# Moving the running counts of a second expert router from VectorE to GpSimd

## What is computed

```python
x = x + _L1_xattn_ref(_layernorm(x, axis=-1), ctx_768, ...)
x = x + _L1_ffn_ref(_layernorm(x, axis=-1), L1_ffn_Wg, ...)

scores = jax.nn.softmax(xf @ Wg.T, axis=-1)
expert_weights, expert_indices = jax.lax.top_k(scores, K)
expert_weights = expert_weights / expert_weights.sum(-1, keepdims=True)
gates = (jax.nn.one_hot(expert_indices, E, dtype=xf.dtype) * expert_weights[..., None]).sum(axis=1)
```

## Time and profile before

| | |
|---|---|
| time, median of 3 runs | 917.48 us (917.41 to 917.69) |
| time of the profiled execution | 909.81 us |
| its span, first to last instruction | 908.6 us |
| mean granted TensorE clock | 0.868 |
| TensorE busy | 707.4 us (78% of the span) |
| VectorE busy | 677.9 us (75%) |
| GpSimd busy | 565.0 us (62%) |
| ScalarE busy | 472.4 us (52%) |

### The profile page before, as it was taken

How to read it: one execution, slowest core, us unless ns; L and a number is a source line. 1 busy time by engine, 2 the same in 40 slices (tenths; PEclk the granted TensorE clock), 3 DMA queues, 4 the chain that set the end, 5 groups by cost and what they waited for, 6 DMA issues and landing times. The chain is left out here.

```text
span 908.6 us, 21071 instructions
## 1 busy us (share of the span) xinstructions
PE 707.4 (78%) x6384; PEld 522.0 (57%) x6384; DVE 677.9 (75%) x3212; ACT 472.4 (52%) x1318; POOL 565.0 (62%) x932
## 2 busy tenths in 40 slices
PE   0697898899888899943798269988888865899960
PEld 0364565566686566422575256666666642799960
DVE  6798999999447887686111294798998886699964
ACT  3466666765303554520233464777777741677740
POOL 7688977786647443201777684347777767377770
PEclk9879999998999999976899655998988876899985
DMA  6300123777227877500564500000000013799918
GB/s 147 59 25 9 41 49 63 90 93 100 41 47 282 268 253 253 180 1 7 76 122 114 181 28 1 3 2 23 23 26 25 23 34 118 212 274 266 266 53 277
DMA packets 98830, 94.43 MB, mean 104 GB/s; under 512 B 37511, under 2 KB 82302, under 8 KB 98142
## 3 DMA queue, kind: packets, MB, share of 16 engines
q1 hardware_dynamic: 91268, 79.34, 33.1%
q0 software_dynamic: 6592, 13.58, 6.0%
q10 hardware_dynamic: 858, 0.17, 0.1%
HBM read 47.76 MB, written 43.19 MB: 100 GB/s over the span
## 5 line engine op out<-in xcount | busy, mean ns | idle before, releaser
L2455 POOL DMA_INDIRECT expert_pairs<-e_ys,e_home x78 | 75.4, 967 | 38.4 <-issue 23.5
L1791 POOL TENSOR_SCALAR a_kb<-a_kr,a_m,a_bk 128x128 f32<-128x128 f32 x128 | 57.8, 452 | 44.4 <-ACT a_kr L2032 32.3
L1809 POOL DMA_INDIRECT expert_slots<-r_rows,r_slotu x64 | 63.3, 990 | 30.2 <-DVE r_rows L2189 15.1
L961 DVE MATCH_REPLACE8 work<-m,work 128x64 f32<-128x64 f32 x384 | 75.6, 206 | 0.0
L1533 POOL DMA_INDIRECT ex_rows<-rows,slot_source x32 | 30.7, 961 | 53.3 <-POOLq L1176 43.9
L948 DVE MAX8 m<-work 128x8 f32<-128x64 f32 x384 | 57.0, 208 | 0.0
L1864 PE MATMUL a_pss<-a_kb,a_qt 32*64 32x256 f32 x512 | 41.5, 463 | 13.8 <-ACT a_pp L2017 11.7
L2221 DVE TENSOR_REDUCE a_mx<-a_pss 128x8 f32<-128x512 f32 x64 | 43.8, 685 | 8.1 <-PE a_pss L1864 7.8
L2422 PE MATMUL e_ps<-e_XH,e_wh 128*128 128x256 f32 x156 | 48.1, 308 | 1.5 <-DVE e_XL L2467 1.5
L1585 ACT ACTIVATE ex_hs<-ex_psh,vec 128x512 f32<-128x512 f32 x32 | 22.0, 687 | 49.8 <-PE ex_psh L1566 49.1
L2424 PE MATMUL e_ps<-e_XH,e_wl 128*128 128x256 f32 x156 | 44.6, 286 | 0.0
(11 more groups left out here) (477 smaller groups left out, 2469.5 us busy)
## 6 DMA issues: line engine op xcount, KB each, us to landing
expert_slots<-rt_unfilled SPq DMA_DIRECT2D x151, 130.0 KB, 2.6
ahead<-folded_weights SPq DMA_DIRECT2D x20, 386.0 KB
e_wf<-folded_weights SPq DMA_DIRECT2D x19, 386.0 KB, 4.1
planes<-rt_zeros SPq DMA_DIRECT2D x4, 1024.0 KB
ew<-in_L_ffn_ew SPq DMA_DIRECT2D x16, 256.0 KB, 3.8
pair_y<-expert_pairs SPq DMA_DIRECT2D x16, 256.0 KB, 5.2
e_xr<-expert_slots SPq DMA_DIRECT2D x27, 130.0 KB, 3.2
folded_weights<-fold_done SPq DMA_DIRECT2D x8, 384.0 KB, 4.3
```

Of the source, the lines that this page charges most:

```text
L961: return own.did(dve.match_replace(wk_[x.j][:, h, :], m8[x.j][:, h, r, :], src[:, h, :], TAKEN))
L1791: m = pool.tensor_scalar(kb[a.j][:, :, h, :], k, m4[:, h:h + 1], bk4[:, h:h + 1], ALU.mult, ALU.add)
L1809: pool.indirect_dma_start(G.slots, bass.IndirectOffsetOnAxis(ap=slot[:, b, k, t:t + 1], axis=0), rb[b % NB][:, k, t, :], None).then_inc(se ...
L2455: pool.indirect_dma_start(G.pair, bass.IndirectOffsetOnAxis(ap=home[i % NY][:, k:k + 1], axis=0), ys[i % NY][:, k, :], None).then_inc(kept ...
```

## The change

The four adds become a function `running_counts`. For blocks 0 to 5 GpSimd calls it, at the head of its slot `PLACE`, before the scaled keys, after a wait for the new semaphore `r_chosen`, which VectorE's last instruction on `sel` raises. For blocks 6 and 7 VectorE still makes the adds. The memset of the first count goes to GpSimd too.

```diff
+        def running_counts(eng, step, b):
+
+            for t in range(b * TB, (b + 1) * TB):
+                m = eng.tensor_tensor(run[:, t + 1, :], run[:, t, :], full["sel"][:, t, :], ALU.add)
+                if t + 1 < (b + 1) * TB:
+                    step.then(m)
+            m.then_inc(r["sel"], 1)
...
                 pool.sem_inc(s["zero"], 1)
+                step.did(pool.memset(run[:, 0, :], 0.0))
...
                 def slot_of(x):
                     a = x.by(3)
+                    counted = due(x, PLACE)
+                    if counted is not None:
+                        pool.wait_ge(r["chosen"], counted + 1)
+                        after(pool, r["sel"], counted)
+                        running_counts(pool, step, counted)
                     if a.real():
                         pool.wait_ge(s["k_sb"], a.t + 1)
...
-                dve.memset(run[:, 0, :], 0.0)
...
                 def choose_second(b):
                     w = part(b)
                     largest(b, 1)
-                    step.then(TT(w["sel"], oh[:, b, 0, :, :], oh[:, b, 1, :, :], ALU.add))
-                    for t in range(b * TB, (b + 1) * TB):
-                        m = TT(run[:, t + 1, :], run[:, t, :], full["sel"][:, t, :], ALU.add)
-                        if t + 1 < (b + 1) * TB:
-                            step.then(m)
-                    m.then_inc(r["sel"], 1)
+                    TT(w["sel"], oh[:, b, 0, :, :], oh[:, b, 1, :, :], ALU.add).then_inc(r["chosen"], 1)
+                    if b >= LAST - 1:
+                        dve.wait_ge(r["chosen"], b + 1)
+                        after(dve, r["sel"], b)
+                        running_counts(dve, step, b)
                     step.then(TT(w["d"], w["m1"], w["m0"], ALU.subtract))
```

More of the change, by code:

```diff
@@ L1673, in combination_and_second_attention @@
         r = {n: C.sem("r2_" + n) for n in (
-            "iota", "lg", "var", "root", "rows", "d", "exp", "sel", "ranks", "pos", "counted",
+            "iota", "lg", "var", "root", "rows", "d", "exp", "chosen", "sel", "ranks", "pos", "counted",
             "slot", "gs", "gturned", "gt", "bias", "bias_sum", "dve", "table")}
```

## The result

The changed kernel takes 935.45 us, the median of 4 runs (929.21 to 938.2), against 917.59 for the kernel before (917.41 to 922.72). The ratio is 1.0171 with a 95% interval of 1.0107 to 1.0236: slower by 15.7 us, between 9.8 and 21.7. The forecast was 930.9, +13.4.

What follows compares the result with a forecast made beforehand. Four engines share the stage, VectorE busiest, but GpSimd reaches the adds after TensorE's ranks want them. Block 1's 2.17 plus 11.2 us over four later periods gave 13.4 on 917.48: 930.9 us, range 926.0 to 937.0.

Steps and rivals of the forecast that it cites:

- the head: Point where GpSimd ends a block's last send; 0.89 to 1.49 us after TensorE's ranks in blocks 1 to 5.
- The ring: Loop from GpSimd's first send through its work, adds, ranks and next send: 26.64 us against 23.85; chance 0.84.
- GpSimd's wait of 2.03 us: GpSimd's wait for VectorE's rows before block 2's first send; claimed not to pay for the adds.
- The term of block 1: Block 1's ranks move from 634.93 to 637.10, waiting for GpSimd's adds: +2.17 us.
- Adds and release: GpSimd's four adds, 1.13 us, plus 0.15 until TensorE's ranks start: 1.28 us.
- Ranks to send: From TensorE's ranks to GpSimd's next first send: 5.63 us at the slow clock, 4.86 for block 1.
- Send to next head: GpSimd's work from a block's first send to the end of its last: 19.73 us without a wait.
- the TensorE rival: TensorE's clock stays low for whole blocks, four slots making 29.8 us: 27 us in all, 944 us; chance 0.06.
- The gain costed at nothing: VectorE's adds removed in blocks 0 to 5, 5.6 us, gain nothing; in blocks 1 to 5 its reciprocal awaits the projection.
- Faster: Adds leave the busiest engine and GpSimd is ready in time: gain up to 5.6 us, 912 us; chance 0.05.
- Absorbed: Adds of 1.13 us fit in GpSimd's 2.03 us wait, nothing moves: 917.5 us within 1.8; chance 0.05.
- Dear adds: GpSimd's adds take 1.0 us more in each of five blocks: +5.0, 935.9 us; within range, no separate chance.

Runs made afterwards that it cites:

- e5: Kernel before, VectorE keeping its adds; a GpSimd memset at its slot PLACE raises a semaphore that the ranks of blocks 0 to 5 also await; ratio 1.0111.
- e3: Kernel before, VectorE keeping its adds; GpSimd also makes the same four adds in slot PLACE, into a tile nothing reads; ratio 0.9949.
- e4: Changed kernel with GpSimd's adds one slot earlier, behind the keys and ahead of the previous block's last sends; ratio 0.9997.
- e1: Changed kernel run once more, unaltered; ratio to the kernel before 1.0162.
- e8: Kernel before, with VectorE's four adds of blocks 0 to 5 done twice, the extra ones into a tile nothing reads; ratio 0.9996.
- e12: Second run of e8's kernel, VectorE's adds of blocks 0 to 5 done twice against the kernel before; ratio 1.0020.
- e7: The change for block 3 alone, VectorE adding in all other blocks; 927.86 us against 919.82 for the kernel before.
- e9: Kernel before, with TensorE's input projections moved between the two halves of the scores; ratio 1.0018 from four of twelve runs, median of all twelve 935.05 us.
- e2: Kernel before, with a bare semaphore increment on GpSimd's queue in slot PLACE that the ranks also wait for; ratio 1.0006.
- e11: Kernel before, unaltered, for a second profile; first sends of blocks 0 to 5 lie 118.48 us apart, one run.

## Why the prediction was right

**The place of the loss: right, and shown.** Ranks behind the head in blocks 1 to 5, none in block 0; e5 has most of the loss (8.55 us) without the adds on GpSimd, e3 the adds there without the loss, and e4 has them there in time, without the loss. The ring was part of the prediction; that GpSimd's wait of 2.03 us does not pay for the adds is borne out too, since that wait grew to 3.49.

**The term of block 1 (+2.17).** +2.00 in after's profile, +2.63 in e1's.

**The ring (+2.79, four times: 11.2).** +11.95 in after and +9.93 in e1. The three parts of 26.64 were each nearly right, with errors that cancel in part:

- Adds and release, 1.28 taken: 1.13 in every block. The adds took 1.05 for 1.08, and TensorE followed 0.06 us behind GpSimd's last add; I had taken 0.15 from a wait of TensorE for VectorE. The Trainium skill (GPSIMD Engine Reference, section 3.1) measures a GpSimd add at 1.96 times VectorE's duration for 2048 columns. That ratio does not hold at 8 columns here: an add took 0.204 us on GpSimd, and on VectorE, before, 0.166 as the median and 0.202 as the mean of 24, so the ratio is 1.2 by the median and 1.0 by the mean.
- Ranks to send, 5.63 taken: 5.50 to 5.53, and 4.79 in the block of each profile where the clock was up for part of it (4.86 had been taken for block 1).
- Send to next head, 19.73 taken as unbroken work: 19.79 in block 1, but 20.31, 20.27 and 20.40 after that. Here is the part of the TensorE rival that I had left inside the range. In the slot behind the ranks TensorE is still at its lower clock (granted 0.50 from 676.46 to 679.90), VectorE's next reciprocal comes late, and GpSimd waits for the statistics that VectorE writes after it. In e1 this is seen in one period only (20.24; the others are 19.7 to 19.8). VectorE's and GpSimd's timelines, after:

```profile
679.90 0.96 DVE L2284 RECIPROCAL a_rt<-a_pso 128x128 f32<-128x128 f32 x1 [1.68 <-PE a_pso L1945]
```

```profile
681.43 0.25 POOL L1783 TENSOR_SCALAR r_v<-r_mv 128x4 f32<-128x4 f32 x1 [0.54 <-DVE r_mv L2255]
```

The clock over the whole distance is 0.79, for 0.86 before.

**The gain costed at nothing: right for this change.** In the profile after, VectorE waits 3.2 to 4.5 us for TensorE before the reciprocal of blocks 1 to 5, so its freed 0.93 us could only lengthen that wait. Beyond this change it is open what VectorE's time is worth: e4 cannot show it, since its own ring holds the period at 23.97, and e8 and e12 disagree. Nor is 23.85 us what the other engines need per block. e7 shows 22.6 to 22.8 with VectorE's adds in place, so the period of before is not a floor; it contains a slow slot of TensorE around each block's ranks. The windows (columns of the earlier trace rows) of that slot in before, and of the ranks to send of block 2 in e7:

```profile
655.60:662.40 6.80, 6.25 (x80) 4.83 (x78) 5.92 (x20) 4.29 (x14) 4.90 (x9) 0.50 0.07 22
```

```profile
668.90:674.40 5.50, 4.47 (x57) 3.16 (x54) 5.23 (x18) 3.98 (x13) 3.90 (x7) 0.93 0.08 27
```

That the slow slot sets the 23.9 fits these two, but e9, meant to show it, changed more than the clock, and e3 speaks against its simplest form: its clock is 0.93 in every one of the five periods, and they are 23.7 to 23.9 all the same. What sets the period of the kernel before stays open.

**The rivals.** Faster fell: no profile shows it. Absorbed fell as the way the change behaves, though e3 shows that its arithmetic (1.1 us fit in 2.03) was true; what it missed is who waits. TensorE as the bound came in part, as above, not as 29.8 us per block (four slots of 7.4 are 29.6, a slip that changes no chance). Dear adds fell: an add took 0.204 us for the 0.21 taken.

**The size.** 13.4 predicted; 13.95 and 12.56 in the two profiled distances; 15.7 (9.8 to 21.7) and 14.9 (9.3 to 20.4) in time. The agreement within 1 us owes something to errors of opposite sign, in the ring and, in e1, between block 1 and the ring. The statement that a measurement can tell 0.2% from no change was wrong: the three runs then known lay 0.3 us apart, but the interval came out at 0.6% to either side. The median of 935.45 lies inside 926 to 937, but two of its four runs, 937.25 and 938.2, do not. The signs named in the forecast are there, roughly: idle before the ranks 2.8 us in block 2 and 2.0 to 2.2 in blocks 3 to 5 (some 3 said), before the reciprocal 3.8 to 4.5 in blocks 2 to 5 (about 4), periods of 26.45 to 27.03 (26.6).

## What to carry to other kernels

Before giving work to an engine because it is idle, find where in its program it is idle and who waits for the new result: GpSimd had 2 us free per block, but behind the point where it would have to deliver. The gap between when the result is wanted and when the engine reaches that place is the price, once per turn of any loop that runs through both. Work taken from the busiest engine is worth nothing while that engine waits for another in the same loop. To find out what its time is worth otherwise, doubling the work there is a cleaner test than moving it, since moved work can close a ring of its own, as in e4; and it takes more than one profile, as e8 and e12 show.

## What was not expected of the hardware

- **A bare semaphore increment on GpSimd's queue does not wait for the work in front of it.** In e2 it stood behind an indirect send that ran from 665.70 to 666.67, and TensorE, which waited for it, started at 665.21. With the increment tied to a memset of 0.11 us, TensorE started 0.26 us behind the end of the send (e5).
- **A block's period differs from execution to execution, and TensorE's clock is only part of it.** Unaltered, the kernel shows periods from 22.89 us (mean granted clock 0.98) to 24.39 (0.80) in one execution (e11). But e3 has 23.9 at 0.93, and e8 and e12, which are the same kernel, lie 5.5 us apart over five periods, with the longer distance at the higher clock (0.88 against 0.86).
- **One profile is one execution.** The first row of the second attention lay at 511 us in one profile of before and at 526 in the other, with nothing changed; a single pair of profiles would have charged 10 us of it to the change.
